# The end of self-attention in a two-layer decoder: zeros by a load, two tiles of low halves, and an earlier row of maxima

## The reference

```
def attn_layer(x, wq, wk, wv, wo, g, b):                  # end of block 1
    q, k, v = (x @ w).reshape(Bsz, T, 16, 64)             # for wq, wk, wv
    scores = einsum('bqhd,bkhd->bhqk', q, k) * 64 ** -0.5
    scores = where(tril, scores, -inf)
    w = softmax(scores)
    o = einsum('bhqk,bkhd->bqhd', w, v).reshape(Bsz, T, 1024)
    return layer_norm(o @ wo + x, g, b)

def _L0_xattn_ref(query, key, value, ...):                # block 2: 16 heads of 16 features
    Q, K, V = query @ W_q.T + b_q, key @ W_k.T + b_k, value @ W_v.T + b_v
    qk = einsum('bhqd,bhkd->bhqk', Q, K) / sqrt(16)
    out = einsum('bhqk,bhkd->bhqd', softmax(qk), V)
    return out @ W_o.T + b_o

x = x + _L0_attn_ref(_layernorm(x), ...)
x = x + _L0_xattn_ref(_layernorm(x), ctx_1024, ctx_1024, ...)
x = x + _L0_ffn_ref(...); x = x + _L1_attn_ref(...); x = x + _L1_xattn_ref(...); x = x + _L1_ffn_ref(...)
```

## Time and profile before

| | us |
|---|---|
| median of 3 runs (lowest, highest) | 1249.07 (1248.18, 1254.14) |
| the profiled execution, its own time | 1250.04 |
| span of its instructions | 1248.2 |
| TensorE busy | 1113.7 (89% of the span) |
| VectorE busy | 795.8 (64%) |
| ScalarE busy | 707.1 (57%) |
| GpSimd busy | 714.3 (57%) |

### The profile page before, as it was taken

How to read it: one execution, slowest core, us unless ns; L and a number is a source line. 1 busy time by engine, 2 the same in 40 slices (tenths; PEclk the granted TensorE clock), 3 DMA queues, 4 the chain that set the end, 5 groups by cost and what they waited for, 6 DMA issues and landing times.

```text
span 1248.2 us, 21861 instructions
## 1 busy us (share of the span) xinstructions
PE 1113.7 (89%) x7155; PEld 879.0 (70%) x7155; DVE 795.8 (64%) x1827; ACT 707.1 (57%) x2030; POOL 714.3 (57%) x776
## 2 busy tenths in 40 slices
PE   3999999999969999999988599984799999977983
PEld 3888888888857888888866477763466666656762
DVE  6778887888843666666675588876332333314795
ACT  2768777777833655555554588880223443225873
POOL 3598898989760225243353677760467555642664
PEclk9999999999989999999999899995899999998995
DMA  4201010000002000000020124610622222221001
GB/s 149 124 18 31 18 12 28 8 29 18 17 1 68 1 2 1 2 1 2 2 60 10 60 88 143 254 35 17 154 43 46 47 44 43 44 44 58 1 26 43
DMA packets 40225, 55.87 MB, mean 45 GB/s; under 512 B 8416, under 2 KB 35040, under 8 KB 38592
## 3 DMA queue, kind: packets, MB, share of 16 engines
q1 hardware_dynamic: 31392, 44.38, 10.9%
q0 software_dynamic: 8736, 10.25, 5.2%
HBM read 42.88 MB, written 11.74 MB: 44 GB/s over the span
## 4 chain that ended last, share of the span: by engine, by line
PE 45%; issue 7%; ACT 7%; DVE 7%; POOL 3%; DMA 1%; POOLq 0%; ACTq 0%; DVEq 0%
PE bank L1577 11%; PE bank L1594 5%; ACT x_prob L1244 4%; PE bank L44 4%; PE bank L46 3%; PE bank L45 3%; PE bank L704 2%; PE bank L732 2%; PE bank L715 2%; PE bank L1334 1%; PE bank L1586 1%; PE bank L1347 1%; PE bank L1284 1%; PE bank L2063 1%; POOL a_prob L871 1%
## 5 line engine op out<-in xcount | busy, mean ns | idle before, releaser
L440 DVE SCALAR_TENSOR_TENSOR ssm_conv<-bank,conv_w,ssm_conv 128x508 f32<-128x508 f32 (+2 forms) x240 | 160.8, 732 | 27.5 <-ACT ssm_conv L356 27.5
L765 ACT ACTIVATE a_prob<-a_prob,a_neg_max 128x128 f32<-128x128 f32 x256 | 99.7, 391 | 117.8 <-DVE a_neg_max L811 117.8
L1577 PE MATMUL bank<-expert_raw,x_kept_next_t 128*128 x312 | 148.7, 600 | 1.2 <-ACT x_kept_next_t L1656 1.2
L871 POOL TENSOR_TENSOR a_prob<-a_prob,a_inv 128x512 f32<-128x512 f32 x64 | 66.5, 1040 | 138.9 <-DVE a_inv L816 138.9
L552 POOL TENSOR_TENSOR ssm_u_lo<-ssm_conv,ssm_u_hi 128x512 fp32r<-128x512 f32 x80 | 101.4, 1289 | 27.0 <-ACT ssm_conv L366 26.9
L1521 POOL DMA_INDIRECT x_rows<-e_y,e_index x39 | 62.9, 1612 | 75.6 <-ACT e_y L1684 71.9
L1244 ACT ACTIVATE x_prob<-bank,x_neg_max 128x128 f32<-128x128 f32 x256 | 89.7, 401 | 11.5 <-DVE x_neg_max L1221 11.5
L1800 DVE COPY e_h_t<-bank 128x512 f32<-128x512 f32 x39 | 27.0, 691 | 105.4 <-PE bank L1586 105.4
L44 PE MATMUL bank<-w_out_hi,ssm_u_hi 128*128 128x256 f32 x320 | 92.1, 288 | 1.1 <-POOL ssm_u_lo L552 1.1
L1131 POOL TENSOR_TENSOR x_prob<-x_prob,x_inv 128x512 f32<-128x512 f32 x64 | 67.0, 1052 | 42.0 <-DVE x_inv L1225 41.5
L46 PE MATMUL bank<-w_out_hi,ssm_u_lo 128*128 128x256 f32 x320 | 90.8, 284 | 0.0
(11 more groups left out here) (338 smaller groups left out, 3264.4 us busy)
## 6 DMA issues: line engine op xcount, KB each, us to landing
expert_raw<-in_experts_laid SPq DMA_DIRECT2D x8, 1536.0 KB, 8.2
attn_raw<-in_attn_w_laid SPq DMA_DIRECT2D x1, 4096.0 KB, 12.4
w_in_raw<-in_L_attn_in_proj_w SPq DMA_DIRECT2D x5, 640.0 KB, 5.9
w_out_raw<-in_L_attn_out_proj_w SPq DMA_DIRECT2D x5, 512.0 KB, 3.9
x_res<-in_x SPq DMA_DIRECT2D x4, 512.0 KB, 5.5
x_res<-in_x SPq DMA_DIRECT2D x1, 2048.0 KB, 8.7
x_context<-in_ctx_t_laid SPq DMA_DIRECT2D x8, 256.0 KB, 4.0
z_rows<-x_kept_next_z SPq DMA_DIRECT2D x8, 256.0 KB, 2.2
```

Of the source, the lines that this page charges most:

```text
L440: op = dve.scalar_tensor_tensor(out=acc, in0=xs, scalar=conv_w[:, c, TAPS - 1 - back:TAPS - back], in1=acc, op0=ALU.mult, op1=ALU.add)
L765: e = act.activation(prob[:, m % 4, i, :], prob[:, m % 4, i, :], ACT.Exp, bias=neg_max[:, m % 4, i:i + 1], accum_out=total[:, m % 4, i:i + 1])
L871: pool.tensor_tensor(prob[:, t % 4, :, :], prob[:, t % 4, :, :], inv[:, t % 4, :].unsqueeze(2).broadcast_to([P, 4, P]), ALU.mult).then_inc ...
L1577: mm = pe.matmul(bank[:, :], rows_t[:, t % 2, k, :], W[:, bass.ds(at + (column + k * FFN), FFN)], start=(k == 0), stop=(k == KD - 1))
```

## The change

1. `clear_v` goes from GpSimd. Instead SyncE's queue loads a tensor of zeros, `noughts` (128 partitions by 2048 numbers, 1 MB), into `x_v`, behind the wait for the last projection job and ahead of the load of `x_bo`. `copy_v` waits for this load.
2. The low halves get a second tile, taken by turns with the first: the first quarter of the second chunk of the low activations `act_t_lo`, which self-attention has read by then. The low half of a unit waits for the output product of the unit two before. Cross-attention keeps that memory free (`low_halves`).
3. `split_at` moves the split of units 30 and 31, on ScalarE and VectorE, from ticks 67 and 69 to 66 and 68. On ScalarE this changes no order. On VectorE the low half of unit 30 then stands in front of the add of unit 29, and that of unit 31 in front of the add of unit 30.
4. `LEAD` becomes {71: 2000}: behind tick 71 everything of the tables below 2000 is issued. That is the maxima of sequence 0 for row groups 0, 1 and 3, which then stand in front of the norm of sequence 15 (tick 72).
5. The add of the second octet also waits until the normed row of two sequences before is written (`z_ready`), since both use one buffer of `a_res`.

```diff
+    o_t_lows = (o_t_lo[:, :, :], ACT_T[LO][:, 1, 0:OCT * P].rearrange("p (c k) -> p c k", c=OCT))
...
+    def split_at(m):
+
+        early = m in (TICKS + SPLIT - 5, TICKS + SPLIT - 3)
+        unit = behind(m, SPLIT - 1 if early else SPLIT)
+        return unit if early or not unit or unit[0] < TICKS // 2 - 2 else None
...
-                    mm = product(pe, Y(U), [o_t_hi[:, U % 2, c, :], o_t_lo[:, c, :]], [x[:, octet * OCT + c, :] for x in wo],
+                    mm = product(pe, Y(U), [o_t_hi[:, U % 2, c, :], o_t_lows[U % 2][:, c, :]], [x[:, octet * OCT + c, :] for x in wo],
...
-            unit = behind(m, SPLIT)
+            unit = split_at(m)
...
-                if U > 0:
-                    dve.wait_ge(y_ready, U)
-                dve.tensor_tensor(o_t_lo[:, :, :], OT(U).rearrange("p (i k) -> p i k", i=OCT),
+                if U > 1:
+                    dve.wait_ge(y_ready, U - 1)
+                dve.tensor_tensor(o_t_lows[U % 2], OT(U).rearrange("p (i k) -> p i k", i=OCT),
...
+                if octet and b >= 2:
+                    dve.wait_ge(z_ready, b - 1)
...
-EARLY_TICKS = {"clear_v": (56, 56), "selections": (57, None), ...
+EARLY_TICKS = {"selections": (57, None), ...
-LEAD = {72: 0}
+LEAD = {71: 2000}
...
         sp.wait_ge(attention["job_ready"], attention["jobs"])
+        sp.dma_start(v[:, :, :, :, :].rearrange("p g a s d -> p (g a s d)"), io["noughts"]).then_inc(v_cleared, 16)
...
-            if phase == "clear_v":
-                if n == 0:
-                    pool.wait_ge(attention["job_ready"], attention["jobs"])
-                    pool.memset(v[:, :, :, :, :], 0.0).then_inc(v_cleared, 1)
-            elif phase == "invert":
+            if phase == "invert":
...
-                    dve.wait_ge(v_cleared, 1)
+                    dve.wait_ge(v_cleared, 16)
...
+    laid["noughts"] = np.zeros((P, 4 * PAIR * D), np.float32)
```

More of the change, by code:

```diff
@@ L935 @@
 BEHIND = 2
-EARLY_TICKS = {"clear_v": (56, 56), "selections": (57, None), "measure": (56, 59), "invert": (56, 59), "norm": (57, 60), "project_k": (57, 61), "copy_k": (57, 61),
+EARLY_TICKS = {"selections": (57, None), "measure": (56, 59), "invert": (56, 59), "norm": (57, 60), "project_k": (57, 61), "copy_k": (57, 61),
                "copy_k_odd": (57, 61), "project_v": (58, 62), "copy_v": (58, 62), "turn_z": (59, 63), "copy_z": (59, 63),
                "project_q": (60, 64), "copy_q": (60, 64)}
-LEAD = {72: 0}
+LEAD = {71: 2000}
 def early_turns(m, phases):
@@ L986, in stage_cross_attention @@
     v = sb(low, "v", [P, 2, 2, PAIR, D])
+    sb(low, "low_halves", [P, OCT * P])
     o, bo, stats = sb(low, "o", [P, KD, P]), sb(low, "bo", [P, D]), sb(low, "stats", [P, SEQS, 6])
     wk, wv, wq, wo = (t.rearrange("p (k n) -> p k n", k=KD) for t in (w[:, 0, :], w[:, 1, :], w[:, 2, :], w_o[:, :]))
-    sb(low, "rest_3", [P, ACT_T_COLS - 26 * D - 6 * SEQS])
+    sb(low, "rest_3", [P, ACT_T_COLS - 26 * D - 6 * SEQS - OCT * P])
     mem["expert_raw"] = high.enter_context(nc.sbuf_tensor("expert_raw", [P, EXPERTS * EXPERT_COLS], F32))
@@ L1377, in stage_cross_attention @@
         "vector": ("selections", "measure", "copy_k", "copy_q", "copy_v", "maxima", "invert_sums", "copy_probs", "copy_out", "add", "measure_next", "norm_next", "copy_next", "copy_logits"),
-        "gpsimd": ("clear_v", "invert", "norm", "share_out", "add_bias", "invert_next")}
+        "gpsimd": ("invert", "norm", "share_out", "add_bias", "invert_next")}
     steps = {"tensor": tensor, "scalar": scalar, "vector": vector, "gpsimd": gpsimd}
```

## The result

The changed kernel took 1243.61 us (median of 6 runs, 1241.28 to 1244.64) where the kernel before took 1250.41 beside it (6 runs, 1248.18 to 1254.21): a ratio of 0.9942, with a 95% interval of 0.9925 to 0.9960, or 7.3 us less (5.0 to 9.4). The forecast was 1243.8, within 1240.8 to 1248.2. The profiled execution took 1243.95 over a span of 1242.1, against 1250.04 and 1248.2.

The account below looks back on a forecast made before the run. Bounds: GpSimd's clearing holding VectorE at tick 56, TensorE's waits in the last ticks, and the last norms ahead of sequence 1's scores. 1.65 + 3.68 = 5.3 us off the median of 1249.07 gives 1243.8, range 1240.8 to 1248.2.

Parts of the forecast that it names:

- The clearing: Tick 56: without GpSimd's clearing, VectorE's masked scores end 1.15 us earlier and bias columns save 0.5 more; 1.65 in all.
- the rival that it wasn't the clearing's: Tick 56: VectorE's hold has another cause, so only the last ticks gain; 1245.4 us, chance 0.10.
- The load of zeros: SyncE's 1 MB load lands before the copy of the values needs it, at 651.1; hidden, cost 0.
- The second tile and the early split: Last ticks: unit 30's output product starts 0.79 us earlier and unit 31's 3.26 earlier.
- The maxima in front: Last norms: first exponential 4.85 us earlier, first scaling 2.78, scores of sequence 1 3.68, with GpSimd late next.
- Waits for `z_ready`: Wait added to 14 adds on VectorE: bounds 0 to 0.2 us, taken as 0.
- Gain taken back later: Rival: a later step takes the last ticks' gain back, leaving only the clearing's part; 1247.4 us, chance 0.08.
- The clock stays low: Rival: TensorE stays at 1.2 GHz for some 9 us more dense work, costing 7.4; 1251.2 us, chance 0.04.
- the sum: Whole change: 1.65 us at the clearing plus 3.68 in the last ticks, 5.3 in all.

Follow-up runs that it names:

- e1: Kernel before the change, with only the clearing taken from GpSimd and made by the load of zeros; 1245.59 us, ratio 0.9964.
- e2: Changed kernel with the clearing back on GpSimd at tick 56, without the load of zeros; 1246.26 us, ratio 0.9966.
- e3: Kernel before the change, with GpSimd's clearing two ticks later, at 58; 1249.30 us, ratio 0.9982.
- e5: Changed kernel with the split of units 30 and 31 at their old ticks, two tiles of low halves kept; 1246.22 us, ratio 0.9960.
- e6: Changed kernel with one tile of low halves again, the earlier split kept; 1243.27 us, ratio 0.9936.
- e4: Changed kernel with the maxima of sequence 0 behind the last norm again; 1246.10 us, ratio 0.9964.
- e7: Changed kernel with GpSimd's bias row adds of sequences 13 to 15 issued with that of sequence 12; 1242.30 us, ratio 0.9932.
- e8: e7 with GpSimd's first two scalings of sequence 0 issued ahead of the last norm's gain and add; 1242.10 us, ratio 0.9924.
- second profile: Changed kernel, unedited, run and profiled again beside e4, e5 and e7; 1242.80 us, ratio 0.9929.
- before_again: Kernel before the change, unedited, profiled once more; that execution took 1254.21 us.

## Why the prediction was right, and which term was mis-sized

*The clearing.* Right, in mechanism and size: masked scores end 1.15 earlier from t56 (5.50 to 4.35), as forecast; the columns shrank by 0.57 (1.01 to 0.44) for a forecast of 0.5. The add still holds the variance, as taken: 641.72 + 0.65 = 642.37 is the end of the add, 641.63 + 0.72 = 642.35. e1, e2 and e3 move the hold with the clearing, so the rival that it wasn't the clearing's fell.

*The load of zeros.* Right: hidden. Its landing of 7.6 us is below the nearest row's 8.7, and the copy of the values starts 12.93 us behind t56, as forecast (651.1 less 638.10 is 13.0). The 128-partition bias row queued behind it landed in 7.3 for 4.0, with no one waiting.

*The second tile and the early split.* Right, to 0.1 us at every step of the table. e5 and e6 show their parts: the split 1.92, the tile 1.33, which overlap, since without the split the tile does nothing in the last ticks: unit 31's output product starts 5.94 behind the last mean in e5, as before.

*The maxima in front.* Right, with the turn that the prediction gave: exponentials 4.88 earlier, scaling only 2.80, GpSimd the one late. e4 shows what that edit is worth, 1.88, and e7 that GpSimd's norms set the release: 0.7 us less in a step of its chain moved the scores of sequence 1 by 0.81. Of the kernels with both low tiles, the exponentials release sequence 1 only in e4 and e8.

*Waits for `z_ready`.* No idle time at any of the last adds is put down to it; 0, as taken.

*Gain taken back later.* No profile shows it: from the scores of sequence 1 to the end it is 543.4 and 544.8 in the two profiles after and 544.4, 546.4 and 543.4 in the three before. A difference of 1 us there means nothing, since over all 13 profiles this stretch lies between 543.4 and 546.4, with every edit of the experiments ahead of it. *The clock stays low:* it did not in the changed kernel. The low spell around the transposes is 691.3 to 701.6 after, 10.2 us, as long as in its second profile and as in the trace before (697.2 to 707.5). In the other two profiles of before it lasted 17.1 us; the scores of sequence 2 then start 10.0 behind those of sequence 1, and not 9.6.

*The mis-sized term* is the clock, put at 0 in both directions. The median fell by 7.3 (5.0 to 9.4), the sum said 5.3. The interval holds 5.3, but the profiles show where further gain can lie. From t56 to the scores of sequence 1 it is 66.6 in the mean of the three profiles before and 59.3 in that of the two after, 7.3 less; 5.5 of it is left (1.74 and 3.8) where the two kinds of low spell that follow are taken out. First, TensorE's second-pair queries, eight matmuls, take 3.08 to 3.48 us in a low spell and 1.89 without; keys' copies to last mean is then 36.4 to 36.6 or 34.9. The spell stands in all four profiles with the clearing at tick 56 (three of before, e2) and in two of the eight of kernels that load the zeros (after and e1). In those two it starts at 674.3, ahead of the queries, which take 2.18 and 2.15, and the whole stretch is as long, 36.41 and 36.38. e3, with the clearing two ticks later, has none. TensorE in before_again and in the second profile of the changed kernel:

```profile
677.97 3.48 PE L1300 MATMUL bank<-x_z_t,x_w 128*128 128x256 f32 x8
```

```profile
675.41 1.89 PE L1307 MATMUL bank<-x_z_t,x_w 128*128 128x256 f32 x8
```

Second, the spell of 691 to 695, worth 1.2. Third, executions of one kernel come in groups by mean granted clock: of 62 of the kernel before beside the experiments, 42 lie between 1248.0 and 1250.7 at 0.953 to 0.957, 19 between 1251.2 and 1254.4 at 0.948 to 0.950, and one at 1265.8; of 12 of the changed kernel none is that far above the others (1241.3 to 1244.6). Three of the six executions of before behind the 7.3 are of the upper group. Against the lower group alone (median 1249.4) the changed kernel's 12 executions (median 1243.2) are 6.2 less. e1 has five runs near 1250.7 (0.950) and six near 1245.2 (0.955 to 0.958), 5.5 apart for the same instructions. Such a group is as large as the whole forecast. That the hold and the wait for the low half bring the spells on fits some of these counts. But e1 lost the hold and has a spell at the queries, and e1, e3 and e5 keep the wait and have none at the product, in one profile each. So what brings the spells on stays open, as does how much of the 2.0 us between 5.3 and 7.3 they explain.

The best times, e7's and e8's, are not told from the changed kernel's: their intervals overlap with 0.9929 (0.9911 to 0.9948).

## What to carry to other kernels

Before a write-only GpSimd instruction is put "where GpSimd is idle", look at what VectorE runs at that time. Three rows that end together name a hold better than their starts do, and a load can replace the instruction where a DMA queue has room. When a step is pulled forward at the end of a stage, follow each chain that feeds the next stage separately; here exponentials came 4.9 us earlier and the scaling 2.8, and only the later one counted until the next experiment turned them round. And where TensorE stands between two clocks, take three profiles of both kernels before a microsecond or two is given to a cause.

## What was unexpected of the hardware

- A VectorE instruction held by GpSimd can lose twice in a row: in e2 the variance started at 640.72 while the add ran to 641.36, and was held on through the clearing from 641.29 to 643.10; in e3 the columns at 646.20 through the scaling and then the clearing, for 2.18 us where it takes 0.44 in the changed kernel.
- What stands behind the held instruction shows as long itself. Two copies out of a bank had 1.77 us in e3, and 0.99 in the changed kernel, and the masked scores 1.83 in the earlier trace rows. The Trainium skill (SBUF — State Buffer, "Who interferes with whom") says that a VectorE instruction with at most one input in SBUF, outside the two-port modes, does not contend with GpSimd. The masked scores, with one input in a bank and one in SBUF, agree with it if their end of 643.60, 0.01 behind the held variance's, is read and not their start.
- Identical programs met low clock in different places: the three profiles of before have it at 677 to 681, and two of them also at 691 to 695 and 831 to 835.
